# A graph network's attention layer: two transposed tables get semaphores of their own, one is loaded a group ahead, and a bias add moves to an earlier sweep

## The chip, the cores and the metric

The kernel runs on one core of a Trainium2 chip. The metric is device time in microseconds (us). The engines are PE (TensorE: matrix products, results in PSUM), PEld (its weight loads), DVE (VectorE), ACT (ScalarE), POOL (GpSimd, which here issues the indirect DMAs that gather rows) and SP (SyncE, which issues plain DMAs in the order of its program and waits on semaphores between them).

## The reference

Four graph layers run one after the other on 6250 nodes with 256 features and 100000 edges, each followed by a layer norm of its result plus its input. The change touches the border between the third (a GRU) and the fourth (graph attention with 4 heads of 64 features):

```python
def gat_layer(x, src, dst, W, att_src, att_dst, bias):
    h = (x @ W).reshape(n, H, F)
    a_src = jnp.sum(h * att_src[None], axis=-1)
    a_dst = jnp.sum(h * att_dst[None], axis=-1)
    e = jax.nn.leaky_relu(a_src[src] + a_dst[dst], 0.2)
    m = jax.ops.segment_max(e, dst, num_segments=n)
    ex = jnp.exp(e - m[dst])
    denom = jax.ops.segment_sum(ex, dst, num_segments=n)
    alpha = ex / (denom[dst] + 1e-16)
    out = jax.ops.segment_sum(h[src] * alpha[..., None], dst, num_segments=n)
    return out.reshape(n, H * F) + bias
...
# src and dst hold the edges and one self loop per node
y = gat_layer(x, src, dst, W, att_src, att_dst, bias) + x
y = (y - mu) / jnp.sqrt(var + 1e-05) * ln_gamma + ln_beta
return jax.nn.relu(y)
```

The weights alpha of the edges that end at one node, its self loop among them, sum to 1.

## The kernel before

The nodes stand in NT = 49 buckets of 128. The edges are sorted by the bucket of their destination and cut into NCH = 832 chunks of 128 edges of one bucket; U = 16 chunks make a trip of the earlier sweeps, GR = 8 chunks make one of NGR = 104 groups of the attention sweep. Each layer's sweep goes once over all chunks: POOL gathers the 128 source rows of a chunk with one indirect DMA, PE multiplies them by a 128x128 one-hot matrix of destinations and DVE adds the product to the bucket's rows.

During the fourth of these sweeps the GRU of finished buckets runs between the chunks (`gru_steps`), and one bucket later the product with the attention matrix W. DVE copies that product (`features`, in PSUM) to `A`, and SP stores it with the nodes' logits to `att_d`. In the same sweeps the one-hots are kept for the attention: as they are (`marks_d`), turned (`turned_d`, 512 KB a group) and, in bf16, as "misses" (`miss_d`, 256 KB a group: where a chunk's edge does not hit a node).

The attention sweep has these steps for a group k of 8 chunks, on PE in the order of the loop `for i in range(NGR + 3)` with positions j = 0 to 7, one chunk a position:

- POOL gathers the chunks' rows of `att_d` into one of GBUF = 5 buffers. A buffer is free when the chunk that used it has been weighed (`s_mm3`).
- `logit_rows(k)`, at i = k-1 and j = 4, turns the source logits; it needs all 8 gathers of group k (`s_parts`).
- `spread(c)`, at i = k, lays the logits of a chunk over all nodes of the bucket, plus minus infinity where `miss` says that the edge does not hit: one 512-column product (L1495) and four of 128 columns (L1500), into one of three PSUM banks. DVE reduces each to a maximum (`reduced`, L2061) and joins it to `max_l` (`maxed`, L2068).
- `own_logits(k)`, at i = k+1 and j = 2 and 3, takes each edge's destination logits out with `ohT`, the turned one-hots (L1510, 8 small products). It ends with `s_dm`.
- ACT scales the gathered rows with the edges' weights (L1027), `weighed(c)` on PE (L1524) follows 19 positions after the chunk's `spread`, and DVE adds the result to `A` (`added`, L2074).

`miss` and `ohT` have two buffers each. SP loads group k of `miss`, then of `ohT` (`turned_in`), then of the marks (`marks_in`), in that order, each after a wait for its buffer. `miss` and `ohT` of one parity signal the same semaphore, and `spread` waits for both:

```python
pe.wait_ge(s_turned_moved[k % 2], turned_out + 32 * (k // 2 + 1))
```

After the sweep ("the ending"), DVE goes over seven batches of seven buckets: it adds the self loops, the scaled sums, x and the bias, takes the layer norm, and a second one with ACT; SP stores each batch.

Of the kernel before, what the change touches and what calls it, by code (L numbers as in the profile page):

```python
# [126 lines left out]
def program(nc, a, out):  # L127
    ctx = ExitStack()
    with ctx:
# [3 lines left out]
        def sem(name):  # L133
            return ctx.enter_context(nc.semaphore(name))
# [300 lines left out]
        s_oht_row = sem("s_oht_row")  # L435
        s_turned_moved = [sem(f"s_turned_moved{k}") for k in range(2)]
        turned_out = 32 * (NGR // 2)
        s_marks_moved = [sem(f"s_marks_moved{k}") for k in range(OHR // GR)]
        marks_out = (16 * (NCH // 8), 16 * (NCH // 8), 0)
        s_spread = sem("s_spread")  # L440
# [113 lines left out]
        def _(sp):  # L554
# [87 lines left out]
                sp.dma_start(att_d[bass.ds(bucket * P, P), :], A[:, bass.ds(bucket, 1), 0:W4].rearrange("p o d -> p (o d)"))\  # L642
                    .then_inc(s_att_out, 16)

            def turned_in(k):
                b = k % 2
                if k > 1:
                    sp.wait_ge(s_spread, GR * (k - 1))
                sp.dma_start(miss[:, b, :], miss_d[k]).then_inc(s_turned_moved[b], 16)
                if k > 1:  # L650
                    sp.wait_ge(s_dm, k - 1)
                sp.dma_start(ohT[:, b, :], turned_d[k]).then_inc(s_turned_moved[b], 16)

            def marks_in(k):
                n = OHR // GR
# [5 lines left out]
            for b in range(2):  # L661
                sp.wait_ge(s_turned_moved[b], turned_out)
                sp.wait_ge(s_marks_moved[b], 16 * (NCH // 8))
            sp.wait_ge(s_att_row, NT)
            for k in range(NGR):
                turned_in(k)
                marks_in(k)
            sp.wait_ge(s_add3, NCH)
# [414 lines left out]
        def _(pe):  # L1083
# [402 lines left out]
            def spread(c):  # L1486
                k, j = c // GR, c % GR
                if j == 0:
                    pe.wait_ge(s_turned_moved[k % 2], turned_out + 32 * (k // 2 + 1))
                    pe.wait_ge(s_ltc, k + 1)  # L1490
                n = len(SP_BANKS)
                if c >= n:
                    pe.wait_ge(s_red, c - n + 1)
                o = ps[:, SP_BANKS[c % n], :]
                pe.matmul(o.rearrange("p (h e) -> p h e", h=H), big_ident[:, :],  # L1495
                          miss[:, k % 2, P * j:P * (j + 1)].rearrange("p (o e) -> p o e", o=1).broadcast_to([P, H, P]),
                          start=True, stop=False, skip_group_check=True)
                for h in range(H):
                    at = H * j + h
                    ins = pe.matmul(o[:, h * P:(h + 1) * P], pick[:, at:at + 1].broadcast_to([kr, P]), spread_t[:, k % 2, :],  # L1500
                                    start=False, stop=(h == H - 1), skip_group_check=True)
                ins.then_inc(s_spread, 1)

            def own_logits(k, buckets, lo, hi):
                if lo == 0:
                    pe.wait_ge(s_maxed, GR * (k + 1))
                    if k:
                        pe.wait_ge(s_own_row, k)
                for j in range(lo, hi):
                    ins = pe.matmul(ps[:, 6, 2 * H * j:2 * H * (j + 1)], ohT[:, k % 2, j * P:(j + 1) * P],  # L1510
                                    node_l[:, bass.ds(buckets[j], 1), H:3 * H].rearrange("p o h -> p (o h)"),
                                    start=True, stop=True)
                if hi == GR:
                    ins.then_inc(s_dm, 1)
# [30 lines left out]
        def _(dve):  # L1545
# [424 lines left out]
            def gru_steps(j, t, u, bt, bu):  # L1970
                if t is not None or u is not None:
                    link.ended()
                if u is not None:
                    features = ps[:, 7, D:2 * D]
                    if j == 2:
                        dve.wait_ge(s_root1, u + 1)
                        link.begin(dve.reciprocal(mv1[:, 1:2], mv1[:, 1:2]))
                    if j == 3:
                        dve.tensor_scalar(tile_at(X, bu), tile_at(X, bu), mv1[:, 0:1], mv1[:, 1:2],
                                          ALU.subtract, ALU.mult).then_inc(s_norm, 1)  # L1980
                    if j == 9:
                        dve.wait_ge(s_prod[7], 1 + u + 1)
                        dve.tensor_scalar(tile_at(A, bu), features, 1.0, None, ALU.mult)
                        link.begin(dve.tensor_tensor(
                            att_tmp.rearrange("p (s d) -> p s d", s=2),
                            features.rearrange("p (o d) -> p o d", o=1).broadcast_to([P, 2, D]), att_st, ALU.mult))
                    if j == 10:
                        dve.sem_inc(s_evac[7], 1)
                        link.begin(dve.tensor_reduce(tile_at(node_l, bu, 2 * H),
                                                     att_tmp.rearrange("p (h f) -> p h f", f=F), AX, ALU.add))  # L1990
                    if j in (11, 12, 13, 14, 15):
                        own = tile_at(node_l, bu, H)
                        part = [A[:, bass.ds(bu, 1), W3 + k * H // 2:W3 + (k + 1) * H // 2].rearrange("p o h -> p (o h)")
                                .bitcast(BF16) for k in range(PARTS)]
                    if j == 11:
                        dve.tensor_scalar(A[:, bass.ds(bu, 1), D:W3].rearrange("p o h -> p (o h)"), own, 1.0, None, ALU.mult)
                        link.begin(dve.tensor_scalar(part[0], own, 1.0, None, ALU.mult))
                    if j == 12:
                        link.begin(dve.tensor_tensor(rest[:, 0, :], own, part[0], ALU.subtract))
                    if j == 13:  # L2000
                        link.begin(dve.tensor_scalar(part[1], rest[:, 0, :], 1.0, None, ALU.mult))
                    if j == 14:
                        link.begin(dve.tensor_tensor(rest[:, 1, :], rest[:, 0, :], part[1], ALU.subtract))
                    if j == 15:
                        dve.tensor_scalar(part[2], rest[:, 1, :], 1.0, None, ALU.mult).then_inc(s_att_row, 1)
                if t is not None:
                    if j == 5:
                        dve.wait_ge(s_prod[6], 1 + t + 1)
                        link.begin(dve.tensor_tensor(hn, ps[:, 5, D:2 * D], b_hn, ALU.add))
                    if j == 6:  # L2010
                        dve.wait_ge(s_gates, 1 + t + 1)
                        link.begin(dve.tensor_tensor(hn, hn, gates[:, 0:D], ALU.mult))
                    if j == 7:
                        dve.tensor_tensor(inn, ps[:, 5, 0:D], hn, ALU.add).then_inc(s_cand, 1)
                    if j == 10:
                        dve.wait_ge(s_tanh, t + 1)
                        link.begin(dve.tensor_tensor(hn, tile_at(X, bt), inn, ALU.subtract))
                    if j == 11:
                        link.begin(dve.tensor_tensor(hn, hn, gates[:, D:2 * D], ALU.mult))
                    if j == 12:  # L2020
                        link.begin(dve.tensor_tensor(hn, hn, inn, ALU.add))
                    if j == 13:
                        link.begin(dve.tensor_tensor(tile_at(X, bt), tile_at(X, bt), hn, ALU.add))
                    if j == 14:
                        dve.sem_inc(s_stat_begun, 1)
                        link.begin(dve.bn_stats(stats1, tile_at(X, bt)))
                    if j == 15:
                        dve.sem_inc(s_stat_begun, 1)
                        link(dve.bn_aggr(mv1, stats1))
                        dve.tensor_scalar(mv1[:, 1:2], mv1[:, 1:2], EPS, None, ALU.add).then_inc(s_var1, 1)  # L2030
# [166 lines left out]
            for i in range(TI + 1):  # L2197
                if i < TI:
                    a, x = batch(A2, i), batch(X, i)
                    own_h = own[i].rearrange("p t (h f) -> p t h f", h=H)  # L2200
                    dve.wait_ge(s_own_in[own_part(i)], 16 * sum(own_part(b) == own_part(i) for b in range(TI)))
                    link(dve.tensor_tensor(own_h, own_h, by_head(batch(ex_l, i)), ALU.mult))
                    dve.wait_ge(s_share, i + 1)
                    link(dve.tensor_tensor(a, a, own[i], ALU.add))
                    link(dve.tensor_tensor(a, a, x, ALU.add))
                    link(dve.tensor_tensor(a, a, over_batch(bias3), ALU.add))
                    first = spread_of(0, i, lambda j: A[:, TU * i + j, 0:D])
                if i:
                    x, y = batch(X, i - 1), own[i - 1]
# [33 lines left out]
```

## Time and profile before

| what | us |
|---|---|
| median of 3 runs | 7747.83 (7735.52 to 7780.11) |
| the profiled execution's own time | 7759.3 |
| its span, first to last instruction | 7757.3 |
| PE busy | 6270.8 (81%) |
| DVE busy | 4847.9 (62%) |
| POOL busy | 5056.3 (65%) |
| ACT busy | 2447.4 (32%) |

The shares are means over stages with different limits. What the change can be worth is read from the stretch of the attention sweep and from the ending, in the rows below.

### The profile page before, as it was taken

What the parts mean: (1) busy time and instruction counts of PE and PEld (TensorE: products, weight loads), DVE (VectorE), ACT (ScalarE), POOL (GpSimd) and SP (SyncE); (2) the same over time, 40 slices, a digit from 0 to 9 for tenths busy, and PEclk for the clock granted to TensorE, in tenths of its full rate; (3) what the DMA queues carried; (4) which work ended last, traced back from release to release, by engine and by line L of the source; (5) the groups of instructions that cost most, each with busy time, mean ns of one, the idle gap of its engine ahead of it and who ended that gap; (6) DMA issues with size and microseconds to landing.
All of it is one profiled execution on the core that took longest, in us unless ns stands there. A gap on an engine that the chain in (4) does not pass through costs nothing.

```text
span 7757.3 us, 105260 instructions
## 1 busy us (share of the span) xinstructions
PE 6270.8 (81%) x25864; PEld 3867.7 (50%) x25864; DVE 4847.9 (62%) x16599; ACT 2447.4 (32%) x7538; POOL 5056.3 (65%) x5303
## 2 busy tenths in 40 slices
PE   8987888889888888888887666668888868888880
PEld 5545555544455554444444444444555546666660
DVE  7986555545455554444444555545777768878878
ACT  3651111112111111011112222221222227777766
POOL 3657777720477776777776777767777757666650
PEclk9998988889899999899998778877999989989995
DMA  1004333344455556455556777773333456666662
GB/s 58 3 20 130 105 105 105 105 89 151 138 159 157 157 158 137 135 157 158 157 158 180 247 240 243 243 215 114 112 111 111 112 106 219 221 199 212 214 181 66
DMA packets 559179, 1141.73 MB, mean 147 GB/s; under 512 B 111895, under 2 KB 304380, under 8 KB 558462
## 3 DMA queue, kind: packets, MB, share of 16 engines
q0 software_dynamic: 249024, 659.51, 32.4%
q1 hardware_dynamic: 195886, 366.27, 13.3%
q10 hardware_dynamic: 113680, 109.21, 4.1%
q8 instruction: 233, 3.82, 0.2%
q14 instruction: 356, 2.92, 0.1%
HBM read 822.31 MB, written 312.26 MB: 146 GB/s over the span
## 4 chain that ended last, share of the span: by engine, by line
PE 37%; POOL 20%; DMA 18%; issue 12%; DVE 11%; ACT 1%; DVEq 1%; ACTq 0%; SPq 0%; POOLq 0%
POOL g L722 20%; PE ps L1112 13%; DMA g<-rel_d,edges 9%; DMA wt<-turned_d 7%; PE ps L1304 4%; PE ps L1334 3%; PE ps L1524 2%; PE ps L1510 2%; DMA g<-rows_d,edges 2%; DVE AY L1788 2%; PE ps L1495 2%; DVE edges L1655 1%; PE ps L1500 1%; DVE edges L1654 1%; PE ps L1158 1%
## 5 line engine op out<-in xcount | busy, mean ns | idle before, releaser
L722 POOL DMA_INDIRECT g<-rel_d,edges x2496 | 2373.1, 951 | 1231.9 <-issue 649.9
L1788 DVE TENSOR_TENSOR AY<-AY,ps 128x256 f32 (+1 forms) x4160 | 1741.4, 419 | 2279.0 <-PE ps L1112 2261.1
L1112 PE MATMUL ps<-g,rows 128*128 128x256 f32 (+1 forms) x4160 | 1403.8, 438 | 690.9 <-DMA g<-rel_d,edges 243.1
L1112 PE MATMUL ps<-g,oh 128*128 128x256 f32 (+1 forms) x4160 | 1449.8, 454 | 295.8 <-DVE rows L1771 95.7
L1112 PEld LDWEIGHTS ps<-g,rows 128*128 128x128 f32 x4160 | 732.7, 206 | 1296.9 <-issue 574.1
L1112 PEld LDWEIGHTS ps<-g,oh 128*128 128x128 f32 x4160 | 799.1, 219 | 749.4 <-issue 375.8
L722 POOL DMA_INDIRECT g<-rows_d,edges x832 | 798.5, 960 | 280.0 <-issue 221.9
L722 POOL DMA_INDIRECT g<-in_x,edges x832 | 797.2, 958 | 273.9 <-issue 193.0
L1334 PE MATMUL ps<-AY,turned 128*128 128x512 f32 x1568 | 755.1, 605 | 0.9 <-ACT turned L749 0.9
L749 ACT ACTIVATE wt<-ps 128x512 f32<-128x512 f32 (+1 forms) x448 | 250.1, 559 | 1463.0 <-PE ps L1334 1428.3
L2061 DVE TENSOR_REDUCE AY<-ps 128x4 f32<-128x512 f32 x832 | 569.1, 684 | 159.1 <-PE ps L1500 156.6
L1771 DVE TENSOR_SCALAR rows<-col,edges 128x128 f32<-128x128 f32 x2080 | 623.5, 300 | 37.9 <-issue 24.9
L1771 DVE TENSOR_SCALAR oh<-col,edges 128x128 f32<-128x128 f32 x2080 | 630.1, 303 | 23.4 <-DMA marks_d<-oh 18.0
L742 POOL DMA_INDIRECT g<-att_d,edges x336 | 318.6, 948 | 210.4 <-PE ps L1524 91.8
L707 POOL DMA_INDIRECT slots_d<-AY,g x294 | 288.9, 983 | 243.2 <-DVE g L1645 167.2
L749 ACT ACTIVATE AY<-ps 128x512 f32<-128x512 f32 (+3 forms) x421 | 181.3, 445 | 821.4 <-PE ps L1409 783.3
L1495 PE MATMUL ps<-AY,big_ident 128*128 128x512 bf16 x832 | 332.5, 400 | 133.2 <-DMA wt<-turned_d 128.4
L742 POOL DMA_INDIRECT AY<-att_d,edges x336 | 318.6, 948 | 161.8 <-PE ps L1524 99.9
L1334 PEld LDWEIGHTS ps<-AY,turned 128*128 128x128 f32 x1568 | 304.9, 195 | 220.2 <-issue 197.7
L1500 PEld LDWEIGHTS ps<-AY 96*128 96x128 bf16 x3328 | 269.1, 101 | 203.3 <-issue 31.4
L2074 DVE TENSOR_TENSOR AY<-AY,ps 128x260 f32 x832 | 345.8, 416 | 7.2 <-PE ps L1524 5.9
L1304 PE MATMUL ps<-AY,turned 128*128 128x512 f32 x784 | 347.2, 596 | 0.0
(384 smaller groups left out, 9687.2 us busy)
## 6 DMA issues: line engine op xcount, KB each, us to landing
rel_d<-wt ACTq DMA_DIRECT2D x392, 256.0 KB, 2.4
turned_d<-AY SPq DMA_DIRECT2D x104, 512.0 KB
wt<-turned_d SPq DMA_DIRECT2D x104, 512.0 KB
AY<-marks_d SPq DMA_DIRECT2D x104, 512.0 KB
rel_d<-g SPq DMA_DIRECT2D x49, 1024.0 KB, 4.4
g<-rel_d,edges POOLq DMA_INDIRECT x2496, 3.0
marks_d<-oh SPq DMA_DIRECT2D x104, 256.0 KB
marks_d<-rows SPq DMA_DIRECT2D x104, 256.0 KB
```

Of the source, the lines that this page charges most:

```text
L722: pool.indirect_dma_start(out=g[:, j, 0:width], out_offset=None, in_=table, in_offset=bass.IndirectOffsetOnAxis(ap=edges[:, word, c:c + 1] ...
L742: pool.indirect_dma_start(out=group_at(k)[:, j, 0:W4], out_offset=None, in_=att_d, in_offset=bass.IndirectOffsetOnAxis(ap=edges[:, 0, c:c ...
L749: return act.activation(o, v, ACT.Copy)
L1112: ins = pe.matmul(sum_slot(order, j), one_hot_at(j % OHS), g[:, j, 0:width], start=True, stop=True)
L1304: ins = pe.matmul(ps[:, q, :], turned[:, b, k * P:(k + 1) * P], relations[0][:, k, q * 512:(q + 1) * 512], start=(k == 0), stop=(k == KD - 1))
L1334: ins = pe.matmul(ps[:, 4 + q % 2, :], turned[:, 0, k * P:(k + 1) * P], w[:, k, q * 512:(q + 1) * 512], start=(k == 0), stop=(k == KD - 1))
L1495: pe.matmul(o.rearrange("p (h e) -> p h e", h=H), big_ident[:, :], miss[:, k % 2, P * j:P * (j + 1)].rearrange("p (o e) -> p o e", o=1).br ...
L1500: ins = pe.matmul(o[:, h * P:(h + 1) * P], pick[:, at:at + 1].broadcast_to([kr, P]), spread_t[:, k % 2, :], start=False, stop=(h == H - 1) ...
L1771: dve.tensor_scalar(one_hot_at(j % OHS), col[:, :], edges_f[:, 2, k:k + 1], None, ALU.is_equal)\
L1788: dve.tensor_tensor(tile_at(A, t, width), tile_at(A, t, width), sum_slot(order, j), ALU.add)\
L2061: dve.tensor_reduce(red[:, c % REDS, :], ps[:, SP_BANKS[c % len(SP_BANKS)], :].rearrange("p (h e) -> p h e", h=H), AX, ALU.max)\
L2074: dve.tensor_tensor(tile_at(A, t, W3), tile_at(A, t, W3), ps[:, WT_BANKS[c % len(WT_BANKS)], 0:W3], ALU.add)\
```

## The change

1. `spread` of a group waits for the misses alone (`s_miss_in`), and `own_logits` waits for the turned one-hots (`s_turned_in`). The old semaphores keep only the stores of the GRU sweep.
2. SP issues the misses of group k+1 ahead of the turned one-hots of group k.
3. DVE adds `bias3` when it copies `features` to `A` in the GRU sweep; the bias add in the ending's loop is left out. Since the weights alpha of a node sum to 1, the bias comes through the sum unchanged.

```diff
--- before.py
+++ after.py
@@ -435,6 +435,8 @@
         s_oht_row = sem("s_oht_row")
         s_turned_moved = [sem(f"s_turned_moved{k}") for k in range(2)]
         turned_out = 32 * (NGR // 2)
+        s_miss_in = [sem(f"s_miss_in{k}") for k in range(2)]
+        s_turned_in = [sem(f"s_turned_in{k}") for k in range(2)]
         s_marks_moved = [sem(f"s_marks_moved{k}") for k in range(OHR // GR)]
         marks_out = (16 * (NCH // 8), 16 * (NCH // 8), 0)
         s_spread = sem("s_spread")
@@ -642,14 +644,15 @@
                 sp.dma_start(att_d[bass.ds(bucket * P, P), :], A[:, bass.ds(bucket, 1), 0:W4].rearrange("p o d -> p (o d)"))\
                     .then_inc(s_att_out, 16)
 
-            def turned_in(k):
-                b = k % 2
+            def miss_in(k):
                 if k > 1:
                     sp.wait_ge(s_spread, GR * (k - 1))
-                sp.dma_start(miss[:, b, :], miss_d[k]).then_inc(s_turned_moved[b], 16)
+                sp.dma_start(miss[:, k % 2, :], miss_d[k]).then_inc(s_miss_in[k % 2], 16)
+
+            def turned_in(k):
                 if k > 1:
                     sp.wait_ge(s_dm, k - 1)
-                sp.dma_start(ohT[:, b, :], turned_d[k]).then_inc(s_turned_moved[b], 16)
+                sp.dma_start(ohT[:, k % 2, :], turned_d[k]).then_inc(s_turned_in[k % 2], 16)
 
             def marks_in(k):
                 n = OHR // GR
@@ -662,7 +665,10 @@
                 sp.wait_ge(s_turned_moved[b], turned_out)
                 sp.wait_ge(s_marks_moved[b], 16 * (NCH // 8))
             sp.wait_ge(s_att_row, NT)
+            miss_in(0)
             for k in range(NGR):
+                if k + 1 < NGR:
+                    miss_in(k + 1)
                 turned_in(k)
                 marks_in(k)
             sp.wait_ge(s_add3, NCH)
@@ -1486,7 +1492,7 @@
             def spread(c):
                 k, j = c // GR, c % GR
                 if j == 0:
-                    pe.wait_ge(s_turned_moved[k % 2], turned_out + 32 * (k // 2 + 1))
+                    pe.wait_ge(s_miss_in[k % 2], 16 * (k // 2 + 1))
                     pe.wait_ge(s_ltc, k + 1)
                 n = len(SP_BANKS)
                 if c >= n:
@@ -1503,6 +1509,7 @@
 
             def own_logits(k, buckets, lo, hi):
                 if lo == 0:
+                    pe.wait_ge(s_turned_in[k % 2], 16 * (k // 2 + 1))
                     pe.wait_ge(s_maxed, GR * (k + 1))
                     if k:
                         pe.wait_ge(s_own_row, k)
@@ -1980,7 +1987,7 @@
                                           ALU.subtract, ALU.mult).then_inc(s_norm, 1)
                     if j == 9:
                         dve.wait_ge(s_prod[7], 1 + u + 1)
-                        dve.tensor_scalar(tile_at(A, bu), features, 1.0, None, ALU.mult)
+                        dve.tensor_tensor(tile_at(A, bu), features, bias3, ALU.add)
                         link.begin(dve.tensor_tensor(
                             att_tmp.rearrange("p (s d) -> p s d", s=2),
                             features.rearrange("p (o d) -> p o d", o=1).broadcast_to([P, 2, D]), att_st, ALU.mult))
@@ -2203,7 +2210,6 @@
                     dve.wait_ge(s_share, i + 1)
                     link(dve.tensor_tensor(a, a, own[i], ALU.add))
                     link(dve.tensor_tensor(a, a, x, ALU.add))
-                    link(dve.tensor_tensor(a, a, over_batch(bias3), ALU.add))
                     first = spread_of(0, i, lambda j: A[:, TU * i + j, 0:D])
                 if i:
                     x, y = batch(X, i - 1), own[i - 1]
```

The lines of the changed kernel lie up to 7 further down; L1495, L1510 and L2204 are L1501, L1517 and L2211 there. In SP's program the attention sweep's loads begin, before, with these rows (`AY<-miss_d` is the misses' load, `wt<-turned_d` that of `ohT`, `AY<-marks_d` that of the marks):

```order
L649 DMA AY<-miss_d 128x1024 [waits s_marks_moved1,s_turned_moved1,s_att_row,s_marks_moved0,s_turned_moved0]
L652 DMA wt<-turned_d 128x1024
L658 DMA AY<-marks_d 128x1024
L649 DMA AY<-miss_d 128x1024
L652 DMA wt<-turned_d 128x1024
L658 DMA AY<-marks_d 128x1024
L649 DMA AY<-miss_d 128x1024 [waits s_spread]
L652 DMA wt<-turned_d 128x1024 [waits s_dm]
L658 DMA AY<-marks_d 128x1024
```

and in the changed kernel:

```order
L650 DMA AY<-miss_d 128x1024 [waits s_marks_moved1,s_turned_moved1,s_att_row,s_marks_moved0,s_turned_moved0]
L650 DMA AY<-miss_d 128x1024
L655 DMA wt<-turned_d 128x1024
L661 DMA AY<-marks_d 128x1024
L650 DMA AY<-miss_d 128x1024 [waits s_spread]
L655 DMA wt<-turned_d 128x1024
L661 DMA AY<-marks_d 128x1024
L650 DMA AY<-miss_d 128x1024 [waits s_spread]
L655 DMA wt<-turned_d 128x1024 [waits s_dm]
```

The turned one-hots of a group now stand behind the misses of the next group and so behind their wait for `s_spread`.

On PE this is the start of a group of `spread` up to the first of the `own_logits` of the group before, in the middle of the sweep, before:

```order
L1495 MATMUL ps<-AY,big_ident 128x512 [waits s_red,s_ltc,s_turned_moved1]
L1500 MATMUL ps<-AY 128x128 x4
L1524 MATMUL ps<-AY 128x260 [waits s_add3,s_wr_act]
L1495 MATMUL ps<-AY,big_ident 128x512 [waits s_red]
L1500 MATMUL ps<-AY 128x128 x4
L1524 MATMUL ps<-AY 128x260 [waits s_add3,s_wr_act]
L1495 MATMUL ps<-AY,big_ident 128x512 [waits s_red]
L1500 MATMUL ps<-AY 128x128 x4
L1510 ISA [waits s_own_row,s_maxed]
L1510 MATMUL ps<-AY,wt 128x8
```

and in the changed kernel:

```order
L1501 MATMUL ps<-AY,big_ident 128x512 [waits s_red,s_ltc,s_miss_in1]
L1506 MATMUL ps<-AY 128x128 x4
L1531 MATMUL ps<-AY 128x260 [waits s_add3,s_wr_act]
L1501 MATMUL ps<-AY,big_ident 128x512 [waits s_red]
L1506 MATMUL ps<-AY 128x128 x4
L1531 MATMUL ps<-AY 128x260 [waits s_add3,s_wr_act]
L1501 MATMUL ps<-AY,big_ident 128x512 [waits s_red]
L1506 MATMUL ps<-AY 128x128 x4
L1517 ISA [waits s_own_row,s_maxed,s_turned_in0]
L1517 MATMUL ps<-AY,wt 128x8
```

The order is the same. The wait for the turned one-hots has gone from the group's first product to the first of the `own_logits`, three chunks further down, and it is for the group before.

On DVE this is the first batch of the ending, from the product with the self loops' weights, before:

```order
L2202 TENSOR_TENSOR AY<-AY 128x1792 [waits s_dve,s_own_in0]
L2204 TENSOR_TENSOR AY<-AY 128x7x256 [waits s_share,s_dve]
L2205 TENSOR_TENSOR AY<-AY,X 128x7x256 [waits s_dve]
L2206 TENSOR_TENSOR AY<-AY 128x7x256 [waits s_dve]
L2176 BN_STATS stage<-AY 128x6 [waits s_dve]
L2176 BN_STATS stage<-AY 128x6 x6
```

and in the changed kernel:

```order
L2209 TENSOR_TENSOR AY<-AY 128x1792 [waits s_dve,s_own_in0]
L2211 TENSOR_TENSOR AY<-AY 128x7x256 [waits s_share,s_dve]
L2212 TENSOR_TENSOR AY<-AY,X 128x7x256 [waits s_dve]
L2183 BN_STATS stage<-AY 128x6 [waits s_dve]
L2183 BN_STATS stage<-AY 128x6 x6
```

One addition over seven buckets is gone from each of the seven batches.

## Rows read from the trace of the kernel before

**Rows 1.** The page: the chain that ended last, shares by engine and line.

```profile
PE 37%; POOL 20%; DMA 18%; issue 12%; DVE 11%; ACT 1%; DVEq 1%; ACTq 0%; SPq 0%; POOLq 0%
POOL g L722 20%; PE ps L1112 13%; DMA g<-rel_d,edges 9%; DMA wt<-turned_d 7%; PE ps L1304 4%; PE ps L1334 3%; PE ps L1524 2%; PE ps L1510 2%; DMA g<-rows_d,edges 2%; DVE AY L1788 2%; PE ps L1495 2%; DVE edges L1655 1%; PE ps L1500 1%; DVE edges L1654 1%; PE ps L1158 1%
```

**Rows 2.** Busy time by window: sweep, ending, ten groups, one group, last group.

```profile
core 0: us, PE busy (x) PEld busy (x) DVE busy (x) ACT busy (x) POOL busy (x), PEclk, DMA share, GB/s
6366.66:7581.71 1215.05, 1066.33 (x7591) 781.71 (x7591) 1006.74 (x3432) 886.68 (x3847) 778.03 (x821) 0.94 0.66 204
7581.71:7757.30 175.59, 0.00 (x0) 0.00 (x0) 153.03 (x282) 101.17 (x310) 0.00 (x0) 0.51 0.23 73
6702.07:6808.43 106.36, 96.38 (x731) 71.29 (x731) 95.55 (x328) 85.06 (x370) 75.57 (x80) 1.00 0.71 227
6864.19:6879.83 15.64, 15.64 (x73) 11.38 (x74) 8.20 (x26) 7.33 (x31) 6.21 (x8) 0.58 0.46 144
7552.18:7581.71 29.53, 24.82 (x127) 16.14 (x126) 21.59 (x72) 25.05 (x108) 0.00 (x0) 0.94 0.06 19
```

**Rows 3.** Waits, 6366.66 to 7581.71: us in total, times, longest.

```profile
PEld ps L1495 <- DMA wt<-turned_d: 170.1, 93, 7.5
DVE AY L2061 <- PE ps L1500: 156.6, 265, 6.3
PE ps L1495 <- DMA wt<-turned_d: 128.4, 90, 7.1
```

**Rows 4.** Timeline of SP, one group: start us, us, what.

```profile
6812.33 0.33 SPq L658 DMA_DIRECT2D AY<-marks_d  x1
6812.71 0.43 SPq L649 DMA_DIRECT2D AY<-miss_d  x1
6813.62 0.33 SPq L652 DMA_DIRECT2D wt<-turned_d  x1
```

**Rows 5.** Timeline of PE at the start of the group that follows.

```profile
6817.66 0.38 PE L1524 MATMUL ps<-AY 128*128 128x260 f32 x1
6819.52 0.39 PE L1495 MATMUL ps<-AY,big_ident 128*128 128x512 bf16 x1 [1.47 <-DMA wt<-turned_d]
```

**Rows 6.** Waits in ten groups at full clock, 6702.07 to 6808.43.

```profile
PE ps L1495 <- DMA wt<-turned_d: 11.1, 11, 1.5
...
DVE AY L2061 <- PE ps L1500: 6.5, 20, 0.7
```

**Rows 7.** Timeline of POOL: the sweep's first gather and its 81st.

```profile
6352.39 0.95 POOL L742 DMA_INDIRECT g<-att_d,edges  x1 [55.47 <-DMA att_d<-AY]
...
6452.59 0.95 POOL L742 DMA_INDIRECT g<-att_d,edges  x1 [0.30 <-issue]
```

**Rows 8.** Line L742, the sweep's 832 gathers: first and last start; waits.

```profile
L742 POOL DMA_INDIRECT AY<-att_d,edges x336: 941/947/1040, 6372.4 to 7527.8; - x168
...
  PE ps L1524: 233.1, 325
```

**Rows 9.** The page: DMA issues of the earlier sweeps, median us to landing.

```profile
g<-rel_d,edges POOLq DMA_INDIRECT x2496, 3.0
```

**Rows 10.** Timeline of PE: the start of the group that ran at low clock.

```profile
6864.19 0.61 PE L1495 MATMUL ps<-AY,big_ident 128*128 128x512 bf16 x1 [2.81 <-DMA wt<-turned_d]
```

**Rows 11.** The chain that ended last, from 7586: start us, us, what.

```profile
7586.82 6.79 ACT AY L1065 x28
7593.71 2.04 DVE AY L2204
7595.77 2.04 DVE AY L2205
7597.83 2.04 DVE AY L2206
7599.89 2.40 DVE stage L2176 x7
7603.93 2.03 DVE AY L2202
```

**Rows 12.** Lines L2206, L1983, L2009: ns minimum/median/maximum, first and last start.

```profile
L2206 DVE TENSOR_TENSOR AY<-AY x7: 2024/2024/2026, 7597.8 to 7720.6; 128x1792 f32<-128x1792 f32 x7
...
L1983 DVE TENSOR_SCALAR AY<-ps x49: 409/417/425, 5382.7 to 6346.3; 128x256 f32 x49
...
L2009 DVE TENSOR_TENSOR rows<-ps,AY x49: 409/417/424, 5358.5 to 6333.4; 128x256 f32<-128x256 f32 x49
```

## The prediction

> **What bounds the kernel now.** I read the chain first: a load of turned one-hots, `wt<-turned_d`, holds 7% of the span, which is much for a transfer that nobody should wait for [rows 1]. It can only lie in the attention sweep, so I took windows: the sweep fills 1215.05 us, from the first `spread` to the last `added`, and the ending 175.59 us, in which DVE is busy for 153.03 [rows 2]. In the sweep the waits name the culprit: PE idles 128.4 us in 90 pieces before L1495 for that load (its weight loads 170.1 us), and DVE in turn 156.6 us for PE [rows 3]. The reader is to see 90 waits for 104 groups: it happens at nearly every group's start.
>
> One group shows why. SP issues the marks, the misses and then the turned one-hots, at 6812.33, 6812.71 and 6813.62 [rows 4]. PE is through with the group's chunks 0.4 us after 6817.66 and stands 1.47 us until 6819.52 [rows 5]: the turned block took 5.90 us from issue. It could not be issued sooner, since `own_logits` of two groups before empties its buffer only at position 3.
>
> How fast each engine could go comes from ten groups at full clock, 106.36 us or 10.64 each [rows 2]. PE waited 11.1 us of them for the load, so it needs (106.36 - 11.1)/10 = 9.53 us a group. DVE waited 6.5 us for PE, so it needs at most (106.36 - 6.5)/10 = 9.99 us, and its busy time alone is 9.56 [rows 2, 6]. POOL issued its first 80 gathers without hindrance in 6452.59 - 6352.39 = 100.20 us, which is 1.2525 us each and 10.02 us a group [rows 7]. Over the whole sweep its 831 steps took 7527.8 - 6352.4 = 1175.4 us, 11.32 us a group, and it waited 233.1 us for PE to free buffers [rows 8]. So today PE, fed late, sets the pace; POOL is next, 1.30 us a group behind, and DVE is right beside it.
>
> The clock takes its part. The granted clock has a mean of 0.94 over the sweep, so PE ran at the lower of its two levels for 2 x 0.06 = 12%, some 146 us. One such group, after a stall of 2.81 us, took 15.64 us at a mean of 0.58, so 13.1 us of it were low, and PE was busy throughout [rows 2, 10]. It lost 15.64 - 9.53 = 6.1 us, 0.47 us for each low one; 146 us then cost 68. The sum closes: 103.9 groups x 9.53 = 990, plus 128.4, plus 68, is 1186 beside the 1175 of POOL's steps.
>
> **The change part by part.** *The split wait.* A group's first product now waits for the misses alone. They are issued when the last `spread` of two groups before is done, and have 8 positions, 10 us, until they are used. The turned block now stands behind the misses' wait in SP's queue, so it leaves up to some 4 positions later than it could, but it is wanted only at position 2 of the next group, 10 positions or 12.7 us after it leaves; its landing took 5.90 us. The marks leave behind it, at about position 2 as before, and are wanted 17 positions later. Both deadlines have room, and no instruction or byte is added: 104 loads of each kind stay. On PE the new wait at the first of the `own_logits` has the later `spread` products and `weighed` behind it, and DVE behind those; it costs nothing while the turned block has twice its time.
>
> That removes 1.1 us a group and leaves three engines near each other: PE 9.53, DVE 9.56 to 9.99, POOL 10.02. POOL is the floor: 831 x 1.2525 = 1040.8 us, so the last gather could start at 7393.2, 134.6 earlier. The ceiling is the present pace at full clock, 10.64, with the clock's losses gone: 103.9 x 10.64 = 1105.5, 69.9 earlier. Between them I take 10.2 us, three tenths of the way up: PE has half a microsecond of spare time a group, but DVE nearly none, and only three PSUM banks lie between them. It gives 103.9 x 10.2 = 1059.8 us, the last gather at 7412.2, **115.6 us earlier**.
>
> *Behind the last gather.* Now 7581.7 - 7527.8 = 53.9 us pass. With PE waiting for gathers instead, the last one lands after some 3.0 us, as those of the earlier sweeps do [rows 9], `logit_rows(103)` follows, then 4 positions (5.1 us) and the last group with its end, 29.53 us [rows 2]: 37.6, so **16.3 us less**. If the drain kept its length, it would be nothing.
>
> *The clock.* Without the stalls PE's idle time comes in smaller pieces. I take the low stretches as mostly gone; what stays is in the 10.2.
>
> *The bias.* Seven additions of 2.024 us go. Each stands in the chain with 2.04 us, between additions and statistics that wait for one another, with nothing of ACT or DMA between [rows 11, 12]: **14.3 us less**. What could eat it is ACT, which has to deliver two scaled batches in each round of 22 us; it is busy for 101.17 of the 175.59 us, so a round of 20 still covers it [rows 2]. In the GRU sweep a copy of PSUM (417 ns) becomes an addition with PSUM (417 ns for the like L2009), 49 times: nothing, at worst 49 x 0.02 = 1 us [rows 12].
>
> Sum: 115.6 + 16.3 + 14.3 = 146.2, so the span goes from 7757.3 to 7611.1 and the profiled execution from 7759.3 to 7613. That execution lies 11.5 above the median, and the three runs differ by 44.6. In proportion the median would be 7602; if what differs is the stalls that the change removes, it would be 7613. I take **7607**.
>
> **The rivals.**
>
> *The low clock stays.* PE will idle some 0.5 us a group for gathers, and one late gather makes a longer gap; the clock fell after 2.81 us [rows 10]. Then PE loses the 68 us as before, 0.65 a group. It cannot win them back, as DVE leaves 0.03 a group: the pace is 9.99 + 0.65 = 10.6, the last gather comes 74 earlier, and with 16.3 and 14.3 it gives 7757.3 - 105 = 7653 and, for the median, 7648. For it: 146 us of low clock. Against it: the ten groups show eleven stalls of up to 1.5 us and a clock of 1.00 [rows 2, 6].
> The Trainium skill (TensorE: Matmul & The Clock Gate, the HAM clock gate) says that the clock is taken away by idleness and given back by sustained activity. By that a PE that is fed more evenly keeps it; the rows agree.
>
> *PE and DVE hinder each other at about 10.8 a group.* Work is uneven: positions 2 and 3 carry `own_logits` on PE, 5 to 7 the logits on DVE. Then 53 + 16 + 14 go, and it ends at 7670.
>
> *Nothing to gain in the sweep.* `spread` also waits for the turned logits (`s_ltc`), for DVE (`s_red`) and for the misses, and a wait is put down to the last by the profile. If one of them ends with the turned block, only the bias remains: 7733. Against it: the misses are issued 0.91 us ahead of it and are half as large [rows 4].
> The Trainium skill (DMA: Bandwidth & Descriptors, Anatomy of one DMA) gives a fixed 2.0 us plus bytes over 436 GB/s; for 512 KB that is an estimate of 3.2 us. By that rule the turned block would have landed at 6816.8, before PE was ready, and the wait would be another's. The trace does not bear it out: the wait ends 5.90 us after the issue.
> What keeps this rival small is the rows' own account: 512 KB of marks and 256 KB of misses go out 1.3 and 0.9 us ahead of the turned block, so that it is the last of three [rows 4, 5].
>
> *Slower: the turned block comes too late at its new place.* Behind the misses and their wait it has 12.7 us. PE would stop in the middle of a group if it took longer, with everything behind it. Slower than before by 0.5% (39 us) needs a pace above 11.32 + (39 + 14)/104 = 11.8, and with 10 of 8 positions between issue and use that is a landing of 14.8 us. At 16 us the pace is 12.8: 154 more, less 14, about 7888. Against it: the longest stall of all was 7.1 us, behind some 4.5 us of cover, and DMA was busy for 0.71 of the ten groups [rows 2, 3]; at 10.2 that is 0.74.
>
> **How the numbers follow.** Forecast 0.63 (7575 to 7635: from POOL's floor, 7757.3 - 134.6 - 16.3 - 14.3 = 7592, less the runs' spread, up to 10.4 a group); low clock 0.19 (to 7665); hindrance 0.09; nothing in the sweep 0.04; late block 0.02; better than all, 0.03. The range holds the first two, 7577 to 7667, and leaves 0.18 out. Two runs of this kernel can be told apart by about 0.5%, 39 us: faster holds the first three and the last, 0.94; same 0.04; slower 0.02.
>
> **What the changed kernel's profile would show.** Right: L1501 waits for no DMA, L1517 neither; POOL steps 1.25 us nearly throughout and its waits for PE fall from 233 below 60; the last gather starts near 7412; the mean clock is over 0.97; the ending is near 161 us. Wrong: a mean clock of 0.94 still, DVE idle under 0.2 us a group with POOL waiting (then DVE binds), or waits of L1517 for `turned_d`. What would make the prediction wrong is DVE above all: its 9.99 is nearly POOL's 10.02, and both leave no room for the smallest mismatch.

## The result: 1.5% faster, and the profile after

The changed kernel takes 7626.89 us in the median of 4 runs (7626.24 to 7629.87) where the kernel before has 7741.68; the ratio is 0.9846, 95% interval 0.9823 to 0.9869. The forecast was 7607 in a range of 7577 to 7667. The profiled execution took 7627.22 with a span of 7625.3, against 7757.3: 132.0 us less. The medians lie only 114.8 us apart, since the profiled execution of the kernel before (7759.3) lies 17.6 above its median; the terms below are those of the two profiled executions. Of the experiments, one execution of e1 (25490.75 us) and one of e2 (10414.29) fell far out; they stand in the medians given below but not in the ratios.

The chain that ended last, from the page of the changed kernel, no longer holds the turned one-hots that stood there with 7% [rows 1]:

```profile
PE 39%; POOL 19%; DVE 14%; issue 14%; DMA 11%; ACT 2%; DVEq 1%; ACTq 0%; SPq 0%; POOLq 0%
POOL g L728 19%; PE ps L1118 14%; DMA g<-rel_d,edges 9%; PE ps L1310 4%; PE ps L1340 3%; PE ps L1531 3%; PE ps L1517 2%; DVE AY L1795 2%; DMA g<-rows_d,edges 2%; DVE edges L1662 1%; DVE AY L2075 1%; PE ps L1506 1%; PE ps L1501 1%; PE ps L1164 1%; DVE edges L1661 1%
```

The windows of the changed kernel: the attention sweep, the ending, twelve groups in the middle, and groups 101 and 102 (columns as in [rows 2]):

```profile
6360.94:7463.77 1102.83, 1051.18 (x7591) 759.01 (x7591) 1001.18 (x3432) 882.83 (x3847) 776.54 (x821) 0.98 0.73 225
7463.77:7625.30 161.53, 0.00 (x0) 0.00 (x0) 138.88 (x276) 100.63 (x310) 0.00 (x0) 0.51 0.24 80
6705.83:6828.87 123.04, 119.38 (x877) 86.61 (x877) 114.98 (x397) 101.68 (x444) 89.79 (x96) 1.00 0.74 235
7404.07:7434.28 30.21, 25.16 (x147) 17.41 (x148) 19.32 (x67) 16.98 (x75) 4.81 (x6) 0.77 0.92 181
```

The sweep went from 1215.05 to 1102.83 us at a mean clock of 0.98 instead of 0.94, the ending from 175.59 to 161.53. Twelve groups take 123.04 us, 10.25 each. The last row is what the forecast did not see: two groups near the end take 30.21 us, at a clock of 0.77 and with the DMA engines busy for 0.92.

POOL's gathers in the changed kernel: count, first and last start, and what its idle time waited for:

```profile
L748 POOL DMA_INDIRECT g<-att_d,edges x336: 940/946/1027, 6346.7 to 7388.3; - x168
L748 POOL DMA_INDIRECT AY<-att_d,edges x336: 940/946/1075, 6366.7 to 7410.0; - x168
...
  issue: 171.0, 561
  PE ps L1531: 105.7, 270
```

The span's 132.0 us fall into four parts. The first gather comes at 6346.7 instead of 6352.4 [rows 7], 5.7 less, which I count as the spread between executions: e9 and e10, which are the same program up to there, have 6342.6 and 6352.5. From the first to the last gather 7410.0 - 6346.7 = 1063.3 us pass instead of 1175.4, **112.1 less**. From the last gather to the last addition it is 7463.8 - 7410.0 = 53.8 instead of 53.9, **nothing**. The ending gives **14.1**. The sum is 131.9.

SP's timeline over one group of the changed kernel shows the new order:

```profile
6828.19 0.33 SPq L650 DMA_DIRECT2D AY<-miss_d  x1
6828.57 0.43 SPq L655 DMA_DIRECT2D wt<-turned_d  x1
6833.33 0.33 SPq L661 DMA_DIRECT2D AY<-marks_d  x1
```

Misses and turned one-hots leave together, 0.3 us before the next group's first product, and the marks 5 us later. PE waits for the turned one-hots twice in the whole sweep, 2.9 us, both times in the last groups. By the packets of the trace (groups 3 to 95) a turned block's last packet ends 3.9 us after its issue in the median and 5.8 at most, and the first of the `own_logits` stands 13.4 us behind the issue; the misses are there 8.4 us before their first use.

### The profile page after: what moved, and what is told of

It reads as the page before. It is cut to its first block, busy times and chain, and to the rows that moved or that the text cites. A ratio compares the mean times of both kernels' runs of the same rounds, so it can differ in the third digit from the quotient of the medians.

```text
span 7625.3 us, 105254 instructions
## 1 busy us (share of the span) xinstructions
PE 6227.7 (82%) x25864; PEld 3837.4 (50%) x25864; DVE 4828.8 (63%) x16592; ACT 2442.8 (32%) x7538; POOL 5044.9 (66%) x5303
## 4 chain that ended last, share of the span: by engine, by line
PE 39%; POOL 19%; DVE 14%; issue 14%; DMA 11%; ACT 2%; DVEq 1%; ACTq 0%; SPq 0%; POOLq 0%
POOL g L728 19%; PE ps L1118 14%; DMA g<-rel_d,edges 9%; PE ps L1310 4%; PE ps L1340 3%; PE ps L1531 3%; PE ps L1517 2%; DVE AY L1795 2%; DMA g<-rows_d,edges 2%; DVE edges L1662 1%; DVE AY L2075 1%; PE ps L1506 1%; PE ps L1501 1%; PE ps L1164 1%; DVE edges L1661 1%
## 5 line engine op out<-in xcount | busy, mean ns | idle before, releaser
L1118 PE MATMUL ps<-g,rows 128*128 128x256 f32 (+1 forms) x4160 | 1385.5, 434 | 691.6 <-DMA g<-rel_d,edges 241.5
L1033 ACT ACTIVATE g<-g 128x64 f32<-128x64 f32 x1344 | 338.5, 335 | 0.0
```

Of the source, the lines that this page charges most:

```text
L1033: ins = act.activation(row[:, h * F:(h + 1) * F], row[:, h * F:(h + 1) * F], ACT.Copy, scale=row[:, D + h:D + h + 1])
L1118: ins = pe.matmul(sum_slot(order, j), one_hot_at(j % OHS), g[:, j, 0:width], start=True, stop=True)
```

## The experiments

Ten of the twelve kernels ran on chips where every kernel took 14% longer: the kernel before had medians of 8838.52 (e1 to e4), 8802.62 (e5 to e8) and 8852.04 us (e11, e12) there. They are compared with each other and by their ratio to the kernel before in the same place. Only e9 and e10 ran where the kernel before had 7740.86.

### e1_split_only and e2_bias_only: the two parts apart

e1 is the changed kernel with the bias in the ending; e2 is the kernel before with the bias in the GRU sweep. The edit that e1 undoes and e2 makes:

```diff
-                        dve.tensor_scalar(tile_at(A, bu), features, 1.0, None, ALU.mult)
+                        dve.tensor_tensor(tile_at(A, bu), features, bias3, ALU.add)
...
-                    link(dve.tensor_tensor(a, a, over_batch(bias3), ALU.add))
```

> The changed kernel with the bias added in the ending again, as before; semaphores and loads as changed. My account: the sweep is as in the changed kernel (group pace 10.19 us, last gather near 7410) and the ending has 175.6 us instead of 161.3: 7641 us. Rival (the pace owes something to the bias move, through the GRU sweep): the first gather or the pace shifts and the sum of the two parts is not the whole.

> The kernel before with the bias added in the GRU sweep and none in the ending. My account: 14.3 us off the ending, 7727 us, the sweep as before with its 90 waits for turned_d. Rival (ACT takes over as the ending's limit): less than 10 us off.

Measured: 8806.76 us for e1, ratio 0.9968 (0.9951 to 0.9985); 8831.13 for e2, ratio 0.9986 (0.9970 to 1.0001). The ending of e1, and then of e2 (window, us, busy times, clock):

```profile
8619.80:8795.40 175.60, 0.00 (x0) 0.00 (x0) 153.06 (x282) 101.21 (x310) 0.00 (x0) 0.50 0.23 73
```

```profile
8653.20:8814.70 161.50, 0.00 (x0) 0.00 (x0) 138.90 (x275) 100.63 (x310) 0.00 (x0) 0.51 0.25 80
```

The ending obeys the bias alone: 175.60 with it, 161.50 without, 14.1 us, the same as between the two kernels of the change. ACT does not take over. The whole time of e2 could not show 14 us (its interval reaches 1.0001); the window does. The sweep, first gather to last addition, was 1390 us in e1 and 1418 in e2: the split wait is worth something in that place too, but much less than 112 us. The trace of e2 says why: with the old shared semaphore PE waits there for the turned block in 28 pieces, not in 90 as in [rows 3],

```profile
PE ps L1495 <- DMA wt<-turned_d: 26.9, 28, 6.6
```

and these 26.9 us are nearly the 28 between the two sweeps. The times in my expectations do not apply there.

### e3, e5, e11: padding that gathers different rows

832 chunks are laid out for 100000 edges; what is over is padding at the end. Its slots carry source row 0, so that all 128 rows of such a gather are the same row. The edit gives each empty slot its partition's number as row; its one-hot column is empty, so the gathered values are multiplied by zero. (The gather sweeps ahead of the attention are five: one over `in_x`, three over `rel_d`, one over `rows_d`. The GRU runs in the fifth of them, over `rows_d`, and not in the fourth, as the description of the kernel before has it.)

```diff
-            dve.tensor_scalar(edges[:, 0, :], word_i[0], -float(LEAST), 0.0, ALU.add, ALU.max).then_inc(s_prep_dve, 1)
+            link(dve.tensor_scalar(word_f[1], word_i[0], 0.0, prow, ALU.is_equal, ALU.mult))
+            link(dve.scalar_tensor_tensor(edges[:, 0, :], word_i[0], -float(LEAST), word_f[1], ALU.add, ALU.max))
+            dve.sem_inc(s_prep_dve, 1)
```

> The changed kernel, in which the empty slots of the edge table gather row p (the partition's number) instead of row 0; their one-hot columns are empty, so nothing of it counts. Theory A (why nothing was won behind the last gather: the last some 26 chunks are padding, their 128 rows are one and the same row of memory, each packet takes 0.5 us instead of 0.15, the last gathers land some 17 us late, PE stalls and its clock falls): packets stay at 0.15 us to the end, groups 101 and 102 take 10.2 us instead of 17.4 and 12.8, some 16 us less behind the last gather as predicted, and something at the end of each of the five sweeps: 7550 to 7610 us. Rival B (the drain is slow because everything ends at once: loads, clock, the ring): no change, 7627.

> The kernel with padding slots spread over rows, again, since in the first round every kernel, the one before too, took some 8800 us. Theory A (the same-row gathers delay the end of each sweep): packets of the gathers stay at 0.15 us to the end, groups 101 and 102 near 10.2 us, 7550 to 7610 us where the changed kernel has 7627. Rival B: 7627.

> The changed kernel with the padding slots' gathers spread over rows, for the third time, hoping for the place where the changed kernel took 7627. Theory A: the stretch from the last gather to the last addition falls from 54 to some 38 us, groups 101 and 102 take 10 to 11 us, each of the other sweeps hands over 5 to 15 us sooner: 7570 to 7605 us. Rival B (only the packets get shorter, the end of the sweep is held by something else): 54 us stay, 7620 or more.

First what the changed kernel itself shows. The queue of the gathers (q0) in its trace from 7300 to 7380 us: packets, MB, share of 16 engines' time:

```profile
q0 software_dynamic: 2959, 8.40, 36.3%
```

and in the same trace from 7410 to 7426 us, when the last gathers drain:

```profile
q0 software_dynamic: 393, 1.12, 71.2%
```

A packet takes 0.363 x 80 x 16 / 2959 = 0.157 us in the middle and 0.712 x 16 x 16 / 393 = 0.46 us at the end, three times as long for the same size. ACT, which waits for the whole group's gathers before it copies the logits, tells the cost in the changed kernel's timeline:

```profile
7413.73 0.28 ACT L755 ACTIVATE AY<-AY 128x96 bf16<-128x96 bf16 x1 [6.42 <-DMA AY<-att_d,edges]
...
7428.95 0.28 ACT L755 ACTIVATE AY<-AY 128x96 bf16<-128x96 bf16 x1 [5.02 <-DMA AY<-att_d,edges]
```

The last gather was issued at 7409.95 and landed 19 us later, not 3.0. With the padding spread, e11's q0 over its last gathers, 8560 to 8586 us:

```profile
q0 software_dynamic: 767, 2.18, 25.8%
```

This is 0.258 x 26 x 16 / 767 = 0.14 us a packet. The same window of e12, which ran beside it with row 0 in its padding (8580 to 8606 us, 15 of these gathers issued against 16), has

```profile
q0 software_dynamic: 683, 1.95, 64.1%
```

or 0.39 us a packet: with the rows spread the slow packets are gone. The landing obeys too. The gathers' last packet ends 12.5 to 12.8 us after the last gather's start in e1, e7 and e8, which have the changed kernel's order of loads and row 0, and 3.3 to 3.5 us after it in e3, e5 and e11. POOL's first gather of the fifth sweep waits for the fourth sweep's end. In e1, and then in e3:

```profile
5896.59 1.04 POOL L728 DMA_INDIRECT g<-rows_d,edges  x1 [30.16 <-DMA rows_d<-X]
```

```profile
5893.88 1.01 POOL L728 DMA_INDIRECT g<-rows_d,edges  x1 [15.69 <-DMA rows_d<-X]
```

This wait is 13.4 to 15.7 us in e3, e5 and e11 and 29.7 to 31.9 in the seven others of those places. From the last gather to the last addition e3, e5 and e11 have 44.9, 46.7 and 44.9 us, 45.5 on average. The three with the same order of loads and row 0 (e1, e7, e8) have 48.5, 48.6 and 50.0, 49.0 on average; the four with the old order (e2, e4, e6, e12) have 49.4 to 55.0. Measured times: 8787.30 us, ratio 0.9927 (0.9904 to 0.9949); 8746.32, 0.9919 (0.9888 to 0.9949); 8797.60, 0.9940 (0.9923 to 0.9957). Their neighbours with row 0 had 0.9961 and 0.9972 (e4 and e6, which also lack the load ahead). The intervals of e5 and e6 lie apart, those of e3 and e4 just touch; a part of either difference belongs to the load ahead, as the unaltered changed kernel did not run in those places. Theory A holds for the packets, for the late landing, for one handover of some 16 us and for some 3.5 us of the drain, where it had forecast 16; the handovers after the second and third sweep did not move. What it is worth where the changed kernel takes 7627 was not measured, and whether any single repeated row is slow, or this one, no run separates.

### e4 and e6: semaphores of their own, loads in the old order

```diff
-            miss_in(0)
             for k in range(NGR):
-                if k + 1 < NGR:
-                    miss_in(k + 1)
+                miss_in(k)
                 turned_in(k)
```

> The changed kernel with the loads in the old order (misses of k, turned of k, marks of k), but semaphores of their own. Theory A (the split wait does all of it: the misses of a group still leave some 6 positions, 7.6 us, before their use and are 256 KB): within 3 us of 7627, no wait of L1501 for miss_d. Rival B (the misses must be loaded ahead): L1501 waits for miss_d in most groups, pace 10.5 or more, 7650 or more.

> The changed kernel with the loads in the old order, again. Theory A (the split wait does all of it): within 3 us of 7627 and no wait of L1501's product for miss_d. Rival B (the misses must be loaded ahead): waits for miss_d in most groups, 7650 or more.

Measured: 8805.33 us, ratio 0.9961 (0.9946 to 0.9975), and 8778.31, ratio 0.9972 (0.9955 to 0.9989). In e4 PE's matmuls wait for misses only in the last three groups (its timeline, time and wait of a group's first product):

```profile
8563.07 0.60 PE L1499 MATMUL ps<-AY,big_ident 128*128 128x512 bf16 x1 [2.07 <-DMA AY<-miss_d]
...
8580.10 0.61 PE L1499 MATMUL ps<-AY,big_ident 128*128 128x512 bf16 x1 [5.75 <-DMA AY<-miss_d]
...
8594.46 0.61 PE L1499 MATMUL ps<-AY,big_ident 128*128 128x512 bf16 x1 [3.07 <-DMA AY<-miss_d]
```

These are groups 100 to 102, and the three waits, 10.9 us, are all that PE's matmuls had for misses in that sweep. In e6 it is 9.3 us in two waits. So in those places, at 12.6 to 12.8 us a group, the split alone removes the wait and the load a group ahead saves some 10 us at the end, where the padding's slow packets pass. But there the shared semaphore had cost 26.9 us and not 128.4; at 10.2 us a group neither edit was run alone.

For that pace there is only a reading of the kernel before. By the packets of its trace (groups 3 to 95) the misses' last packet ends 4.0 us after the issue in the median, 1.1 us before PE could have begun the group (0.95 us after the start of the last `spread` before it); in 12 of these 93 groups it ends up to 1.2 us later than that. The turned block's last packet ends 0.36 us or more before PE's first product, whose wait it ends; with that lag added, the misses would have held PE in 14 groups, for some 11 us. My estimate is therefore that the split does about nine tenths of the 128.4 us there too, and the load ahead the rest. It is not shown by a run.

### e7, e8, e12: one more DVE addition at position 3 or 6

e7 has this edit, e8 the same with `j == 6`; e12 has both, in different groups, on top of e6's order. The added operation's result is not used.

```diff
+            col2 = X[:, 0, :]
...
+                    if j == 3 and 0 <= k < NGR:
+                        dve.tensor_tensor(stage[:, 0, :], col2, col2, ALU.add)
```

> The changed kernel with one more DVE addition over 256 columns (some 0.35 to 0.43 us) in each group at position 3, where PE has the own_logits products and DVE follows it. It computes nothing that is used. Theory A (PE and DVE take turns in holding the group: DVE alone sets positions 6 to 1, PE alone positions 2 to 5, and together they make 10.19 us): the addition fits into DVE's idle time there; pace 10.2 to 10.35, below 15 us more in all. Rival B (DVE's whole work is the bound, 9.58 busy and gaps that cannot be used): pace 10.55 to 10.6, 38 to 43 us more.

> The same addition at position 6, where DVE carries the logits' small operations. Theory A: all of it shows, pace 10.55 to 10.6, 38 to 43 us more. Rival B: the same. Rival C (POOL's 10.02 a group is the bound and both engines wait for gathers): neither this nor the addition at position 3 shows more than 0.1 us a group.

> The changed kernel with the loads in the old order, and one more DVE addition over 256 columns a group, at position 3 in groups 10 to 49 and at position 6 in groups 55 to 94; it computes nothing that is used. Groups 3 to 9, 50 to 54 and 95 to 99 show the old order alone: 10.2 if the misses need not be loaded ahead, 10.5 or more if they must. Theory A (PE and DVE take turns, and DVE has idle time at positions 2 to 5): groups 10 to 49 at 10.2 to 10.35, groups 55 to 94 at 10.55 to 10.65. Rival B (DVE's whole work is the bound): both at 10.55 or more. Rival C (POOL's 10.02 is the bound): both at 10.2 or 10.3.

All three fell on the slower chips: 8766.59, 8760.08 and 8820.65 us in one run each. Between e7, e8 and e6 (8778.31) on one chip there is no difference that means anything, and in e12 groups 10 to 49 take 12.78 us and 55 to 94 take 13.00, where two kernels with the same order and no addition have 12.84 and 12.83 (e4) and 12.59 and 12.69 (e6). The two differ by 0.14 to 0.25 us between themselves, and e12 stands 0.06 us below to 0.31 above them, so neither place of the addition can be told from the scatter. Whether PE and DVE take turns is open.

### e9_changed_again: the changed kernel once more

> The changed kernel as it is, to have it beside the kernel before in the place where the earlier runs took some 8800 us. Theory A (there every signal from engine to engine is late now and then, all five gather sweeps pace at 11.5 us a group instead of 10.0, and the change saves only what its waits cost there): 10 to 45 us less than before, attention pace 12.7 to 12.9. Rival B (it was the edits of those runs): near 7627 and a pace of 10.2.

Measured: 7632.98 us, before 7740.86, ratio 0.9857 (0.9813 to 0.9900). It fell on a chip like that of the first result, so it confirms the result and leaves rival and theory on the slower chips without a control.

### e10_order_only: the new order with the old wait

```diff
                     pe.wait_ge(s_miss_in[k % 2], 16 * (k // 2 + 1))
+                    pe.wait_ge(s_turned_in[k % 2], 16 * (k // 2 + 1))
```

> The changed kernel's order of loads, but the first spread of a group waits for the turned one-hots of its own group as well, as before the change. Theory A (the slower rival's mechanism: behind the misses' wait the turned block leaves only when the group before is done, so the split wait is what makes the order possible): PE stops some 5 us at every group's start, 104 times, pace 15 us or more, 450 us or more above the changed kernel. Rival B (the loads ahead hide it): no wait, as the changed kernel.

Measured: 8440.89 us in one run, 808 more than e9 on the same chip. The sweep's window, and the waits in it (us in total, times, longest):

```profile
6366.00:8277.50 1911.50, 1442.30 (x7592) 1029.77 (x7592) 1033.65 (x3432) 891.35 (x3848) 780.47 (x821) 0.71 0.42 130
```

```profile
PEld ps L1502 <- issue: 499.3, 103, 7.5
...
PE ps L1502 <- DMA wt<-turned_d: 293.8, 66, 7.1
```

The pace is 18 us a group. Theory A holds, and the price is higher than the least that I gave (450 us): stalls are only half of it. Beside the changed kernel's sweep PE's idle time grows by (1911.50 - 1442.30) - (1102.83 - 1051.18) = 418 us, and its busy time for the same products by 1442.30 - 1051.18 = 391 us, as the clock falls to a mean of 0.71. A stall of some 4 us each group (418/104) costs its length and then about as much again in the low clock behind it.

## Why the prediction was right, point by point

**The removed wait.** Right, and by its mechanism: 128.4 us of PE's waits before L1495 [rows 3] are gone, and no other transfer took their place. e10 shows by one wait, on a chip of the same pace, that this wait is what counts: with the turned block at its new place in the queue, the old wait costs 808 us. How the gain divides between the split and the load ahead is shown only for the slower chips (e4, e6) and estimated for this one. The turned block had the room that the forecast gave it, 13.4 us against 12.7, and landed in 3.9; the slower rival did not occur.

**The pace.** Forecast 10.2 us a group, last gather 115.6 us earlier; measured 1063.3 / 103.9 = 10.23, and 112.1. The 10.2 was a choice between two bounds, 10.02 and 10.64, and not a sum; that it came within 0.04 is partly luck. The floor, POOL's 10.02 [rows 7], was not reached. The reason given for the distance, PE and DVE behind three PSUM banks, fits the chain of one group in the changed kernel (start us, us, what):

```profile
6810.34 0.68 PE ps L1531 x2
...
6811.45 0.85 PE ps L1517 x8
...
6813.28 0.85 PE ps L1517 x8
...
6814.89 0.24 PE ps L1506 x4
6815.22 0.69 DVE AY L2068
...
6817.17 0.15 DVE AY L2075
...
6820.04 0.35 DVE AY L2081
...
6820.52 0.46 PE ps L1531
```

From 6810.34 to 6815.22 the chain stays on PE, through both halves of `own_logits`; from 6815.22 to 6820.52 it stays on DVE, through the logits' small operations; then it is on PE again. 4.88 and 5.30 us make 10.18. Each engine has spare time only while the other leads. This is read from the chain of one group and is not shown; the runs that should have shown it by adding work gave no answer. POOL's waits for PE fell from 233.1 to 105.7 us, not below 60 as forecast: POOL did not become the engine that all waited for.

**The clock.** Right: 0.98 over the sweep, and 1.00 in twelve groups in the middle, with PE fed evenly. e10, which differs by one wait, has 0.71: the clock is lost behind the stalls. The Trainium skill (TensorE: Matmul & The Clock Gate, the HAM clock gate) says that idleness takes the clock and activity gives it back; these two runs agree.

**Behind the last gather: the term that failed.** Forecast 16.3 us less, measured 0.1. The step was "the last one lands after some 3.0 us, as those of the earlier sweeps do". The 3.0 is a median over the gathers of three earlier sweeps, and the same view of the kernel before gives 20.4 as the longest; those at a sweep's end are padding, and the last one here landed after 19.0. What follows the landing took 34.8 us, where the forecast's other terms make 34.6: the landing alone is the missing 16. On the way PE stalled, its clock fell, and group 101 took 17.4 us and group 102 12.8 (together the 30.21 above) instead of 20.4 for both. In the kernel before, groups 99 to 102 took 14.9 to 17.2 us each, POOL stood behind PE up to the end, and the last packet of its gathers ended 7.1 us after the last one's start: its 53.9 us are as long as the 53.8 now, but made up of other parts. e3, e5 and e11 show the cause of the late landing. They do not show that the 16 us come back without it: on the slower chips the landing came 9 us sooner with the rows spread and the drain was shorter by some 3.5, and on the faster one it was not measured.

**The bias.** Forecast 14.3, measured 14.1, by e1 and e2 as well. The addition in the GRU sweep has a median of 419 ns where the copy had 417 [rows 12]: 49 x 0.002 us.

**The sum.** 20 us separate 7607 from 7626.9: 16.2 of the drain, 3.5 of the pace and 0.2 of the ending, less 5.7 by which the sweep began sooner; the remaining 6 come from my discount of 6 us between the profiled run and the median, which the changed kernel does not need, as its runs lie within 4 us. So a mechanism that failed by 16 us and an early start of 5.7 that nobody forecast stand inside the same total: the range was wide enough for both, and the total does not vouch for each term.

**The rule on landing times.** The Trainium skill (DMA: Bandwidth & Descriptors, Anatomy of one DMA) would have had the turned block land before PE was ready. Its fit is given for one DMA issued by GpSimd, and this block is issued by SP behind two others, so the rule was stretched. The runs bear the lateness out: in the kernel before the block's last packet ends 5.0 us after its issue in the median, where the estimate by the page was 3.2, and the wait went when just that block was split off.

## What to carry to other kernels

Two transfers that signal one semaphore are both due when the first is used; if one is used later, give it its own semaphore before you reorder, for a reordering that was made for the split wait is harmful without it (e10). A latency taken as a median says nothing of the end of a loop: look at the last transfers by themselves, above all where they are padding. When three engines are within 5% of each other, do not expect the pace of the slowest one's need: here it stayed 2% above it (10.23 against 10.02).

## What the runs showed that I had not expected

An indirect gather whose 128 indices are all the same row is slow: 0.46 us a packet against 0.157 for the edges' own rows, for packets of the same size; and on one of the slower chips 0.39 against 0.14 when the same slots got different rows.

On the slower chips the operations of POOL, DVE and ACT took as long as ever (busy 5052, 4799 and 2444 us in e12, 5045, 4829 and 2443 in the changed kernel), and PE's took longer in all (6454 against 6228 us) at a lower mean clock (0.84 instead of 0.91); but engines waited for each other longer. In e12's second sweep, where the changed kernel keeps 10.0 us a group and e12 11.6, two of the longest waits are:

```profile
DVE AY L1793 <- remote: 316.2, 70, 8.8
ACT wt L753 <- remote: 285.5, 51, 10.5
```

"remote" is a release that the profile can put down to no engine. What it was stays open.
